# First block of a transformer kernel: the sums with v move between the score products of a step, and a half's keys move next to its queries

## The reference

```
qkv = x @ Wqkv                          # q, k, v: 16 heads of 16
attn = softmax(q @ k.T * (SCALE / TEMPERATURE) * alpha + beta) * gamma
ka = gate(mean(q), mean(k))             # small networks, once per sequence and head
x = layernorm(x + (attn @ (v * (1 + ka))) @ Wproj + bproj)
```

## Time and profile before

| | |
|---|---|
| median of 3 runs | 2671.85 us (2671.34 to 2677.64) |
| the profiled execution | 2680.05 us, its span 2678.1 us |
| mean granted TensorE clock | 0.956 of 2.4 GHz |
| PE busy | 2404.8 us (90%) |
| PEld / DVE / ACT / POOL busy | 1401.3 / 1640.3 / 1235.1 / 713.7 us |
| L213, L221 | 207.0 and 201.5 us, 512 of each |
| L245 | 143.2 us, 1024 |
| L353 on ACT | 279.4 us, 512; 141.6 us idle ahead of it |
| L449 on DVE | 318.1 us, 512; 118.9 us idle ahead of it |

### The profile page before, as it was taken

How to read it: one execution, slowest core, us unless ns; L and a number is a source line. 1 busy time by engine, 2 the same in 40 slices (tenths; PEclk the granted TensorE clock), 3 DMA queues, 4 the chain that set the end, 5 groups by cost and what they waited for, 6 DMA issues and landing times.

```text
span 2678.1 us, 39615 instructions
## 1 busy us (share of the span) xinstructions
PE 2404.8 (90%) x14896; PEld 1401.3 (52%) x14896; DVE 1640.3 (61%) x4283; ACT 1235.1 (46%) x2758; POOL 713.7 (27%) x707
## 2 busy tenths in 40 slices
PE   4789998999879889887689999999999999999996
PEld 1223333333354267666355666666666666666664
DVE  5656667667451055665676667666676677676653
ACT  0455555455421134111366566565556655565530
POOL 1121223231011032111433333323332333333310
PEclk7789999999999989998899999999999999999998
DMA  8132333232413912000000000000000100000001
GB/s 280 39 102 75 105 104 114 81 103 82 145 71 131 421 79 80 17 17 17 26 5 5 2 5 5 5 5 2 28 13 12 42 10 19 5 21 21 19 21 33
DMA packets 70941, 158.38 MB, mean 59 GB/s; under 512 B 6320, under 2 KB 48416, under 8 KB 63168
## 3 DMA queue, kind: packets, MB, share of 16 engines
q1 hardware_dynamic: 68448, 146.68, 15.8%
q0 software_dynamic: 2304, 9.18, 1.5%
HBM read 116.52 MB, written 35.13 MB: 57 GB/s over the span
## 4 chain that ended last, share of the span: by engine, by line
PE 70%; DVE 13%; DMA 6%; ACT 3%; issue 3%; POOL 3%; SPq 1%; POOLq 0%; DVEq 0%; ACTq 0%
PE banks L1788 8%; PE banks L1766 6%; PE banks L1663 6%; PE banks L1675 4%; PE banks L245 4%; PE banks L221 4%; PE banks L213 3%; PE banks L1737 3%; PE banks L1706 3%; PE banks L1748 3%; DMA arena<-stacks 2%; PE banks L1294 2%; PE banks L1721 2%; PE banks L265 2%; DVE arena L2257 2%
## 5 line engine op out<-in xcount | busy, mean ns | idle before, releaser
L449 DVE TENSOR_REDUCE arena<-banks 128x1 f32<-128x512 f32 x512 | 318.1, 682 | 118.9 <-PE banks L213 118.8
L353 ACT ACTIVATE arena<-banks 128x512 f32<-128x512 f32 x512 | 279.4, 595 | 141.6 <-PE banks L221 139.6
L1788 PE MATMUL banks<-arena 128*128 128x512 f32 x640 | 293.3, 594 | 6.1 <-DVE arena L1993 6.1
L1859 ACT ACTIVATE arena<-arena 128x256 f32<-128x256 f32 (+1 forms) x512 | 286.3, 562 | 2.5 <-DVE arena L1957 2.1
L2060 POOL TENSOR_TENSOR arena<-arena 128x512 f32<-128x512 f32 x128 | 162.6, 1271 | 445.1 <-DVE arena L1977 445.1
L213 PE MATMUL banks<-arena 96*128 96x512 bf16 x512 | 207.0, 407 | 56.0 <-DMA arena<-stacks 37.8
L1663 PE MATMUL banks<-arena 128*128 128x512 f32 x512 | 246.9, 606 | 5.0 <-DVE arena L1977 4.2
L1951 DVE CUSTOM_DVE_ANT_0 arena<-banks,arena 128x256 f32<-128x256 f32 (+1 forms) x512 | 169.2, 386 | 83.1 <-PE banks L1706 83.0
L221 PE MATMUL banks<-arena 128*128 128x512 bf16 x512 | 201.5, 396 | 15.6 <-ACT arena L353 10.4
L1788 PEld LDWEIGHTS banks<-arena 128*128 128x128 f32 x640 | 117.7, 190 | 138.3 <-issue 126.9
L2056 POOL TENSOR_TENSOR arena<-arena 128x16 f32<-128x16 f32 x64 | 187.5, 2930 | 5.4
(11 more groups left out here) (290 smaller groups left out, 4374.3 us busy)
## 6 DMA issues: line engine op xcount, KB each, us to landing
arena<-in_e_W SPq DMA_DIRECT2D x32, 1024.0 KB, 12.4
arena<-stacks SPq DMA_DIRECT2D x64, 384.0 KB, 4.4
arena<-in_e_Wg SPq DMA_DIRECT2D x16, 1024.0 KB, 14.7
stacks<-arena SPq DMA_DIRECT2D x32, 384.0 KB, 2.6
stacks<-arena SPq DMA_DIRECT2D x32, 256.0 KB, 3.1
arena<-dens POOLq DMA_DIRECT2D x32, 256.0 KB, 4.6
arena<-in_xT SPq DMA_DIRECT2D x8, 512.0 KB, 10.6
arena<-in_x SPq DMA_DIRECT2D x8, 512.0 KB, 9.9
```

The lines of the kernel that those rows point to most:

```text
L353: e.activation(ex[:, j], self.psum[:, 3 + k % 2], ACT.Exp).then_inc(s["a_e"], 1)
L449: e.tensor_reduce(mx[:, t, j:j + 1], self.psum[:, k % 3], AX.X, ALU.max, negate=True).then_inc(s["a_m"], 1)
L1788: i = e.matmul(bank, weights[:, c], self.hT[:, c], start=c == 0, stop=c == 1)
L1859: k = e.activation(pr[:, h, at:], pr[:, h, at:], ACT.Exp, bias=mx[:, h:h + 1], scale=rn[:, h:h + 1], accum_out=den[:, h:h + 1])
```

## The change

Two things change. TensorE does the sums with v of the step before after the second of the four pairs of score products, and no longer after the fourth. The keys of a half are projected at t = 1 of the even unit, in the step after the queries, and no longer at t = 2; in the same edit SyncE does the tasks of a step ahead of the fetch, so that the fetch at (u, 1) of an even unit stands behind the keys' three transfers.

```
 def tasks1():
                 for side in (0, 1):
-                    at[4 * k + 2 * h, 2 * side].append(("qk", 2 * k + 2 + h, side))
+                    at[4 * k + 2 * h, side].append(("qk", 2 * k + 2 + h, side))
...
 def tensor1(self, e, w):
                     e.matmul(self.psum[:, 3 + k % 2], stack[:, 1, j, t * P:(t + 1) * P], stack[:, 0, j, :],
                              start=True, stop=True).then_inc(s["a_exp"], 1)
-            if before is not None:
-                self.tensor1_values(e, w, *before)
+                if j == 1 and before is not None:
+                    self.tensor1_values(e, w, *before)
...
 def sync1(self, e, w):
+            for task in self.at1[u, t]:
+                self.sync1_task(e, w, *task)
             if t == 1 and u >= 1 and u + 3 < UNITS:
                 self.fetch1(e, w, u + 3)
-            for task in self.at1[u, t]:
-                self.sync1_task(e, w, *task)
```

## The result

The changed kernel takes 2719.88 us, the median of 4 runs (2713.43 to 2725.01), against 2674.74 before on the same chips. The ratio is 1.0168 with a 95% interval of 1.0139 to 1.0196: 45 us slower, where the forecast was 43. The profiled execution is the fastest of the four, 2713.43 us with a span of 2711.5.

The account below looks back on a forecast made before the run. TensorE was taken to bound the kernel, its rare long wait for the fetched stack at a unit's start deciding. Six sequences at +7.6 us, +4.5 and -7 gave +43: 2715 us against the median, range 2680 to 2755.

Parts of the forecast that it names:

- The late fetch: Even units: fetch starts 8.78 (4k + 2) or 10.3 us (4k) after the shift's copy, +3.3 and +4.0 us.
- The queue: A fetch behind 768 KB of stores lands 0.6 us later at each of two even units, +1.2 a sequence.
- The clock: TensorE's clock falls after two longer waits per sequence, 1.3 to 1.5 us each; net +1.6 us a sequence.
- The sums with v: Moved between the pairs: -1.0 and -0.9 us in units 4k, -0.4 per two odd units, -7 at the end.
- The step: With the sums with v between the pairs, a TensorE step gets shorter by about 0.2 us.
- Keys one step earlier: The keys' own product, moved from t = 2 to t = 1, is the same TensorE work before and after.
- VectorE's wait for the sums: VectorE's reciprocal waits for the gather's load behind the keys' cut, ahead of unit 4k + 1's maxima: nothing to 2.09 us.
- the third rival: Much slower: VectorE's reciprocal waits 2 us for the gather, with full clock and queue costs; +77 us, 2749 us, chance 0.08.
- The sum: +7.6 us a sequence, +45.6 for six (units 4 to 27), +4.5 in sequence 0, -7 at the end: +43 us.
- The first rival: Faster: SyncE starts the fetch where it does now, so the gains stand alone, 23 us; 2649 us, chance 0.12.

Follow-up runs that it names:

- fetch_ahead: The changed kernel with SyncE's fetch put back ahead of the keys' stores: 2659.75 us, ratio 0.9954.
- gather_ahead: The changed kernel with the gather at (4k, 1) moved ahead of the keys in the table: 2721.0 us, ratio 1.0177.
- v_mid_only: The kernel before with only the sums with v moved to the middle: 2640.24 us, ratio 0.987.
- fetch_gather_ahead: The changed kernel with both the fetch and the gather moved ahead of the keys: 2637.99 us, ratio 0.987.
- v_at_end: The changed kernel with the sums with v back behind the fourth pair: 2745.73 us, ratio 1.0267.
- fetch_early: The kernel before with the fetch moved to the start of (u, 0), ahead of the queries' stores and the shift: 2676.76 us, ratio 1.0016.

## Why the prediction was right, point by point

**The late fetch** (right, mechanism and size). It was to start 8.78 and 10.3 us after the shift's copy; it starts 8.71 and 10.15 us after it (8.72 in unit 4, which has no turn0, so that the 4.0 us of my sum belong to five of the six sequences). fetch_ahead shows that this is the loss: 60 us, with the gather still behind the keys, and 83 us with the gather ahead. The wait of the unit's first L213 was to be 3 to 5 us at even units. It is 4.1 to 4.6 behind the units 4k + 2 and 5.8 to 6.6 behind the units 4k, so above the forecast there.

**The queue** (right, half the size). I took 0.6 us per fetch. From the fetch's start to TensorE it is now 5.70 in unit 22 against 5.01, and 6.09 in unit 24 against 4.55, so 0.7 and 1.5; the means over units 4 to 27 are 5.94 against 4.99 and 6.42 against 4.99. A part is already in the issue of the two transfers, 1.14 and 1.76 us against 0.77. Not all of the 1.5 is the stores': in gather_ahead, where the gather's transfers stand ahead, the issue takes 1.14 us in unit 24 too, and it is 5.48 us from the start to TensorE. The Trainium skill gives its fixed cost plus bytes at 436 GB/s (DMA: Bandwidth & Descriptors, Anatomy of one DMA) for transfers that GpSimd issues, and these are SyncE's; the 1.8 us estimated by it is above both.

**The clock** (right, about half the size). Stretches of the changed kernel right behind the fetch's wait, the first steps of units 19 and 23 and the start of unit 25, and an undisturbed one (length, PE, PEld, DVE, ACT, POOL, granted clock, DMA, GB/s):

```profile
493.87:499.86 5.99, 5.99 (x25) 2.59 (x25) 3.27 (x5) 2.28 (x4) 0.00 (x0) 0.75 0.00 0
579.95:587.20 7.25, 6.99 (x23) 3.01 (x25) 3.36 (x5) 2.39 (x4) 0.00 (x0) 0.61 0.01 2
627.20:633.90 6.70, 6.62 (x21) 2.42 (x22) 4.27 (x10) 2.39 (x4) 4.12 (x6) 0.54 0.33 99
596.00:600.50 4.50, 4.50 (x26) 2.31 (x25) 2.84 (x6) 2.10 (x5) 0.00 (x0) 1.00 0.22 56
```

The steps (19, 0) and (23, 0) have a proj; at full clock a step with one takes 4.57 us. So the clock, fallen to its lower level of 1.2 GHz, costs 1.4 us in the one and 2.7 in the other, behind waits of 4.38 and 4.12 us. The rows of before had shown 1.3 to 1.5. All six steps of this kind, units 7 to 27, take 5.99 to 7.29 us, in the mean 2.1 above 4.57. I had counted 1.6 us per sequence for both waits of it, net of what fell before; these steps show 1.4 to 2.7 for one. In the changed kernel the first L213 behind each of the twelve waits of over 4 us takes 0.61 us instead of 0.39. The length of a wait alone does not decide, though: in the kernel before, a first step behind 1.95 us (unit 21) ran at 0.70, and one behind 2.00 us (unit 19) at 1.00.

**The sums with v** (right in sign, too small). v_mid_only shows 34 us, where my terms without a fetch penalty came to 23. The wait at the start of a unit 4k fell from 2.09 to 1.19, as forecast. The step was mis-sized. TensorE in the changed kernel, at the end of the steps (23, 2) and (23, 3):

```profile
595.02 1.70 PEld L284 LDWEIGHTS banks<-arena 128*128 128x128 f32 x8
595.24 1.89 PE L284 MATMUL banks<-arena 128*128 128x256 f32 x8
596.96 0.38 PE L213 MATMUL banks<-arena 96*128 96x512 bf16 x1
...
599.59 0.38 PE L221 MATMUL banks<-arena 128*128 128x512 bf16 x1
599.81 1.89 PE L284 MATMUL banks<-arena 128*128 128x256 f32 x8
601.54 0.38 PE L213 MATMUL banks<-arena 96*128 96x512 bf16 x1
```

and the weight load of the proj in the kernel before, step (23, 0):

```profile
552.07 1.59 PEld L284 LDWEIGHTS banks<-arena 128*128 128x128 f32 x8 [0.84 <-issue]
```

The proj enters 0.22 us after the last L221, where I had 0.22 to 0.32, and costs 1.72, where it had cost 1.83 behind the sums (552.08 to the next step at 553.91). It is cheaper where its first weight load starts 0.22 us ahead of it than where the load starts with it. The type of the product ahead does not decide that: in unit 22 of the changed kernel L265 (566.21 to 568.03), whose load waited for the shift's copy, costs 1.82 right behind the bf16 L276, against 1.72 (560.28 to 562.00) with its load ahead. A step with a proj takes 4.57 us here, against 4.93 from 548.98 to 553.91 before, 0.36 less and not 0.2.

**Keys one step earlier** (right). The product itself was to cost nothing; fetch_gather_ahead, 2638, against v_mid_only, 2640, shows it.

**VectorE's wait for the sums** (the third rival). It came, 36.4 us in six places, more than the 2 us each that I gave it. It cost nothing that gather_ahead could show, since it ended with the fetch, and would have cost 22 us otherwise (fetch_gather_ahead).

**The sum.** The six sequences from unit 4 to unit 27, from the first one's shift copy to the copy six sequences later, took 474.5 us before and 520.0 after: +45.5, where the sum says 45.6. That is closer than its terms: against the kernel with neither part, keys and fetch cost 71 us (v_at_end), and 80 on top of the moved sums (the changed kernel against v_mid_only), where my terms give 66, and the sums' move gives 26 to 34 where they give 23. Two errors went opposite ways, and that they met within 2 us is luck. The 45 us are a difference of medians, and single executions scatter by some 10 us: the two profiled ones are only 33 us apart (spans 2678.1 and 2711.5). Outside the six sequences the changed one gains 12 us there, 5.2 ahead of them and 6.9 behind, where my sum has 2.5. The copies stand at 182.58 and 657.09, and at 177.35 and 697.39 us; one row of each kernel, the last:

```profile
657.09 0.59 ACT L359 ACTIVATE arena<-banks 32x512 bf16<-32x512 f32 x1 [0.60 <-PE banks L276]
```
```profile
697.39 0.57 ACT L359 ACTIVATE arena<-banks 32x512 bf16<-32x512 f32 x1
```

**The first rival** (faster, 0.12) was right that the sums' move alone is a gain, 34 us where it had 23, and about where it decides; the fetch is late, so it did not happen. Its wait for the fetch, though, was less of a reserve than I wrote under what bounds the kernel: fetch_early shows that a second chain, the way of the sums through DRAM, ends at nearly the same time.

## What to carry to other kernels

A transfer's place in the list of the engine that issues it is part of its cost. Before a task moves ahead of a fetch, ask what the task waits for, here the keys' product, its copy and four GpSimd instructions of 3.8 us together, and add that to the fetch's start; the answer came out to within 0.15 us. A wait that is long in the trace is not yet a reserve: when two chains end together, removing one shows the other, so the later consumer has to move as well (fetch early: no gain; with the scaling later too: 13 us). Behind the second there can be a third, as the shift's reload showed. A gain should be tried without the part that comes with it: here one half of the change was worth 34 us by itself, and the other by itself lost 71.

## What the runs showed of the hardware

- Two waits of nearly the same length, 4.38 and 4.12 us, cost 1.4 and 2.7 us in the step behind them, by a granted clock of 0.75 and 0.61.
- A wait of 1.95 us was followed by a step at a granted clock of 0.70, one of 2.00 us by a step at 1.00 (units 21 and 19 of the kernel before).
- A float32 product of 8 instructions cost 1.72 us where its first weight load started 0.22 us ahead of it, and 1.82 to 1.83 where the load started with it.
- From the start of two transfers of 384 KB to the product that waits for them it took 5.70 us right behind 768 KB of stores in the same queue, against 5.01 without them, and 6.09 against 4.55 where the gather's transfers ran beside them.
